# Wide-head attention without a loop, with queries, keys and values as split products

## What is computed

```python
DIM = 128; NUM_HEADS = 16; DIM_HEAD = 64; INNER = NUM_HEADS * DIM_HEAD      # 1024
w_q   (DIM, INNER)          queries from the twice normalised x
w_kv  (DIM, 2 * INNER)      keys and values from the context
w_out (INNER, DIM), b_out, gate, ln_gamma, ln_beta
...
def _layernorm(x, gamma, beta, eps=1e-05): ...
SCALE = DIM_HEAD ** (-0.5)
```

## Time and profile before

| | |
|---|---|
| median of 3 runs | 962.73 us (961.08 to 964.19) |
| span of the profiled execution | 1010.8 us |
| own time of the profiled execution | only the span is given |
| TensorE matmul busy | 783.2 us (77%) |
| VectorE busy | 608.2 us (60%) |
| ScalarE busy | 486.4 us (48%) |
| GpSimd busy | 372.9 us (37%) |

### The profile page before, as it was taken

One profiled execution on the slowest core, in us unless ns is written; L12 is line 12 of the kernel. 1 busy time (PEld: TensorE's weight loads), 2 busy tenths in 40 slices (PEclk: granted clock), 3 DMA queues, 4 the chain that ended last, 5 costly groups with the idle time before them and its releaser, 6 DMA issues.

```text
span 1010.8 us, 24129 instructions
## 1 busy us (share of the span) xinstructions
PE 783.2 (77%) x8041; PEld 646.4 (64%) x8041; DVE 608.2 (60%) x1568; ACT 486.4 (48%) x984; POOL 372.9 (37%) x492
## 2 busy tenths in 40 slices
PE   6998899999999789996477775667677559969005
PEld 3766787888888679985476664667676526644005
DVE  3886747777777667767353224632222368867895
ACT  3886434555444344432154435334444357745753
POOL 5663421111111331111566653155556535550810
PEclk9999699999999979999699989579989769978557
DMA  6300000000000000033332213101111300000001
GB/s 187 96 0 1 1 1 3 2 3 0 0 0 3 1 11 19 21 102 103 95 100 88 64 41 105 42 19 43 40 37 45 85 23 3 0 1 1 0 0 42
DMA packets 49218, 36.06 MB, mean 36 GB/s; under 512 B 7665, under 2 KB 44978, under 8 KB 49138
## 3 DMA queue, kind: packets, MB, share of 16 engines
q1 hardware_dynamic: 43420, 24.45, 8.5%
q0 software_dynamic: 4992, 10.23, 3.6%
q10 hardware_dynamic: 726, 0.33, 0.1%
HBM read 26.73 MB, written 8.26 MB: 35 GB/s over the span
## 4 chain that ended last, share of the span: by engine, by line
PE 67%; DVE 9%; another core or an unknown queue 6%; issue 5%; ACT 5%; DMA 3%; DVEq 2%; POOL 2%; ACTq 1%; SPq 1%; POOLq 0%
PE psum L2118 9%; PE psum L1464 7%; PE psum L2143 4%; PE psum L1034 3%; PE psum L976 3%; PE psum L954 3%; PE psum L939 3%; PE psum L2442 2%; PE psum L1431 2%; PE psum L1432 2%; PE psum L1433 2%; PE psum L323 2%; PE psum L1016 2%; PE psum L663 2%
## 5 line engine op out<-in xcount | busy, mean ns | idle before, releaser
L2118 PE MATMUL psum<-E_XT,E_weights 128*128 128x128 f32 x780 | 114.3, 298 | 52.4 <-ACT E_XT L2198 27.7
L2118 PEld LDWEIGHTS psum<-E_XT,E_weights 128*128 128x128 f32 x780 | 103.0, 209 | 61.2 <-ACT E_XT L2198 30.8
L2266 POOL DMA_INDIRECT y_scratch<-E_y,route_place_of x78 | 78.8, 1010 | 83.2 <-DVE E_y L2321 37.8
L2258 POOL DMA_INDIRECT E_rows<-rows_scratch,route_token_of x78 | 76.4, 979 | 32.1 <-issue 25.5
L1723 DVE SCALAR_TENSOR_TENSOR X<-psum,E_gates,X 128x128 f32<-128x128 f32 x256 | 71.7, 344 | 26.5 <-PE psum L1464 26.4
L1464 PEld LDWEIGHTS psum<-E_w,E_h 128*128 128x128 f32 x512 | 69.4, 198 | 11.5 <-issue 3.5
L2221 ACT ACTIVATE E_h<-psum,cols 128x128 f32<-128x128 f32 x156 | 44.5, 368 | 66.4 <-issue 31.3
L1548 ACT ACTIVATE E_h<-psum,cols 128x512 f32<-128x512 f32 x64 | 43.8, 687 | 67.8 <-PE psum L1433 67.7
L1464 PE MATMUL psum<-E_w,E_h 128*128 128x128 f32 x512 | 70.4, 282 | 4.8 <-DVE X L1723 3.8
L2311 DVE TENSOR_TENSOR E_h<-E_sg,psum 128x384 f32<-128x384 f32 x39 | 21.6, 554 | 77.5 <-remote 26.8
L203 POOL TENSOR_TENSOR rstd<-vareps,nhalf 128x4 f32<-128x4 f32 x24 | 24.6, 1029 | 75.0 <-DVE vareps L197 74.9
(11 more groups left out here) (346 smaller groups left out, 2160.2 us busy)
## 6 DMA issues: line engine op xcount, KB each, us to landing
routed_back<-y_scratch SPq DMA_DIRECT2D x16, 256.0 KB, 4.9
E_first<-in_L_xattn_W SPq DMA_DIRECT2D x1, 2048.0 KB, 8.6
L1w<-in_L_xattn_W SPq DMA_DIRECT2D x8, 256.0 KB, 4.7
rows_scratch<-xn SPq DMA_DIRECT2D x8, 256.0 KB, 2.3
E_w<-in_L_ffn_routed_w SPq DMA_DIRECT2D x28, 64.0 KB, 1.9
E_raw<-in_L_ffn_w_down SPq DMA_DIRECT2D x8, 176.0 KB
E_rows<-rows_scratch,route_token_of POOLq DMA_INDIRECT x78
y_scratch<-E_y,route_place_of POOLq DMA_INDIRECT x78
```

The costliest lines, as they stand in the source:

```text
L2118: mm = pe.matmul(out[:, c * P:(c + 1) * P], WE[:, p, (k0 + c) * P:(k0 + c + 1) * P], XT[:, p, :], start=True, stop=True)
L2258: pool.indirect_dma_start(out=xg[:, i % 4, :], out_offset=None, in_=rows[:, :], in_offset=bass.IndirectOffsetOnAxis(ap=disp.token_of[:, i: ...
L2266: pool.indirect_dma_start(out=yrows[:, :], in_=y[:, i % 3, :], in_offset=None, out_offset=bass.IndirectOffsetOnAxis(ap=disp.place_of[:, i: ...
```

## The change

The wide-head layer is written out for all its steps, without a hardware loop, and has 23 steps instead of 21. Keys, queries and values become products of three passes on split operands. Keys and queries are made for a pair of tiles: 256 moving columns, and of the eight blocks of 128 rows four in one step and four in the next (`half`). Values take the 128 context columns of both sequences as the stationary operand at once: 3 matmuls of 512 columns for each half of the heads. J1 then holds the even heads of both sequences and J0 the odd ones, and they are copied by halves of 64 partitions: two copies on VectorE, two on ScalarE.

The high and low parts come from four places. The weights: three copies of 128x1024 by ScalarE (`wide_high`) at the start of the feed-forward layer, and three subtractions by GpSimd (`low_parts`) in that layer, ahead of `owners`; the low part overwrites the weights. The context: four copies of 128x512 by ScalarE and four subtractions by GpSimd at the start of the wide-head layer, ahead of its first rstd. The normalised rows: a second evacuation of turn_x by ScalarE (xH) and a subtraction of 128x128 by GpSimd (xL, signal x_low), which takes the place of the context copy. The keys of the first pair stand ahead of the wait for the layer before. To make room, the weights of the feed-forward layer get a buffer of their own.

The diff, cut to its core:

```diff
+        def three(out, wk, cc, xs, start=True):
+            ws = slice(cc * P, (cc + 1) * P)
+            pe.matmul(out, WH[:, wk, ws], xs[0], start=True, stop=False)
+            pe.matmul(out, WH[:, wk, ws], xs[1], start=False, stop=False)
+            return pe.matmul(out, WL[:, wk, ws], xs[0], start=False, stop=True)
...
+        def turn_x(t, n, p):
+            pe.wait_ge(*xn_ready(t + 1))
+            if n >= 5:
+                pe.wait_ge(*v_odd(n - 4))
...
+        def queries(i, n):
+            pair, half = i // 2, i % 2
+            r = pair % 2
+            pe.wait_ge(*x_low(2 * pair + 2))
+            for j in range(2):
+                if 3 <= n <= NT:
+                    pe.wait_ge(*k_ready(2 * (n - 1) + j + 1))
...
+                for c in range(2):
+                    mm = three((J1, J0)[j][:, c * PW:(c + 1) * PW], 0, 4 * half + 2 * j + c, (xH[:, r, :], xL[:, r, :]))
+                mm.then_inc(q_ps.sem, 1)
...
+        def values(t, n):
...
+                pe.matmul(bank, CH[:, cols], wv[0][:, :, u, :], start=True, stop=False)
+                pe.matmul(bank, CL[:, cols], wv[0][:, :, u, :], start=False, stop=False)
+                mm = pe.matmul(bank, CH[:, cols], wv[1][:, :, u, :], start=False, stop=True)
...
+        for i in range(2):
+            keys(i, 0)
+        m.begin(pe, start)
+
         def step(n, p):
             q = 1 - p
...
+            if is_tile(n - 4):
+                scores(n - 4)
+            if is_tile(n - 1):
+                turn_x(n - 1, n, q)
+            if is_tile(n - 5):
+                turn_probs(n - 5, q)
...
+            if 3 <= n <= NT:
+                keys(n - 1, n)
+            if is_tile(n - 6):
+                turn_out(n - 6, p)
+            if is_tile(n - 2):
+                queries(n - 2, n)
+            if is_tile(n - 5):
+                weigh_values(n - 5, q)
...
+            if is_tile(n - 6):
+                project(n - 6, p)
+            if is_tile(n - 4):
+                values(n - 4, n)
...
     def scalar(act):
+        for s, n in first_products_done:
+            act.wait_ge(s, n)
+        for g in range(NG):
+            cols = slice(g * GW, (g + 1) * GW)
+            act.activation(CH[:, cols], m.ctxT[:, cols], ACT.Copy).then_inc(ctx_high.sem, 1)
...
+                act.wait_ge(*v_ps(2 * n - 6))
+                if n >= 6:
+                    act.wait_ge(*o_ps(n - 5))
+                for b in range(2):
+                    cp = act.activation(v[S:P, p, b].rearrange("p c d -> p (c d)"), J0[b * S:(b + 1) * S, :], ACT.Copy)
+                cp.then_inc(v_odd.sem, 1)
...
     def gpsimd(pool):
+        for g in range(NG):
+            cols = slice(g * GW, (g + 1) * GW)
+            pool.wait_ge(*ctx_high(g + 1))
+            pool.tensor_tensor(CL[:, cols], m.ctxT[:, cols], CH[:, cols], ALU.subtract).then_inc(ctx_low.sem, 1)
         m.begin(pool, start)
...
         def step(n, p):
-            if live(n):
+            if is_tile(n):
                 inner.rstd(pool, n, p, xn_ready)
-            if live(n + 1):
+            if is_tile(n + 1):
                 outer.rstd(pool, n + 1, 1 - p, x1_ready)
-            if live(n - 1):
-                context(n - 1, 1 - p)
+            if is_tile(n - 1):
+                t = n - 1
+                at = slice(t % 2 * P, (t % 2 + 1) * P)
+                pool.wait_ge(*xnT_ready(t + 1))
+                pool.tensor_tensor(xL[:, t // 2 % 2, at], xnT[:, 1 - p, :], xH[:, t // 2 % 2, at],
+                                   ALU.subtract).then_inc(x_low.sem, 1)
...
         if beside:
+            spec["pool_between"](pool)
             for j in range(NCH):
                 beside.owners(pool, j)
...
+        def low_parts(pool):
+            for i, k in enumerate((1, 0, 2)):
+                pool.wait_ge(wide_high_ready, i + 1)
+                pool.tensor_tensor(m.wide_low[:, k, :], wide[:, k, :], m.wide_high[:, k, :], ALU.subtract
+                                   ).then_inc(wide_low_ready, 1)
...
+            for k in (1, 0, 2):
+                act.activation(m.wide_high[:, k, :], wide[:, k, :], ACT.Copy).then_inc(wide_high_ready, 1)
```

More of the change, by code:

```diff
@@ L919, in wide_head_attention, with steps, is_tile @@
     L.done = x_done(NT)
[L920 to L927, removed]
+    END = NT + 7
+    first_products_done = m.split_free
+    after = m.stats_after.get
+    def steps(step):
+        for n in range(END):
+            step(n, n % 2)
+    def is_tile(t):
+        return 0 <= t < NT
     def tensor(pe):
-        m.begin(pe, start)
         pe.wait_ge(*m.dispatch.owner_ready(1))
-        def keys(t, p):
-            for j in range(2):
[L935 to L940, removed]
-                mm.then_inc(k_ps.sem, 1)
[L943 to L950, removed]
-                else:
[L952 to L955, removed]
-                mm.then_inc(v_ps.sem, 1)
[L958 to L983, removed]
@@ new lines, in step, with keys_kept @@
+            if after(tag) and n == NT + 5:
+                after(tag).turn(pe, 1)
+            if is_tile(n - 6):
+                project(n - 6, p)
+            if is_tile(n - 4):
+                values(n - 4, n)
+        steps(step)
+    def scalar(act):
+        for s, n in first_products_done:
[3 more added lines that the diff above has]
+            act.activation(CH[:, cols], m.ctxT[:, cols], ACT.Copy).then_inc(ctx_high.sem, 1)
+        def keys_kept(i):
+            pair, half = i // 2, i % 2
+            if pair >= 2:
+                act.wait_ge(*scores_ready(2 * pair - 2))
+            for j in range(2):
+                c = 4 * half + 2 * j
+                act.wait_ge(*k_ps(2 * i + j + 1))
+                act.activation(kT[pair % 2][:, c:c + 2, :].rearrange("p c k -> p (c k)"), (J1, J0)[j],
+                               ACT.Copy).then_inc(k_ready.sem, 1)
+        for i in range(2):
+            keys_kept(i)
@@ L1134, in gpsimd @@
         outer.rstd(pool, 0, 0, x1_ready)
[L1135 to L1136 removed]
+        steps(step)
+        if after(tag):
             for g in range(NG - 1):
[L1138 removed]
+                after(tag).rstd(pool, g)
             for g in range(2):
[L1140 to L1141 removed]
+                after(tag).low_part(pool, g)
+                after(tag).residual(pool, g)
     def vector(dve):
```

243 lines of the change are left out of this document (135 added, 108 removed).

## The result

The changed kernel takes 980.12 us (median of 4 runs, 979.38 to 983.59), the kernel before 963.15 beside it (961.08 to 964.19): ratio 1.0185, 95% interval 1.0154 to 1.0217, 17 us slower. Predicted were 977.5 (960 to 990), slower.

The account below looks back on a forecast made before the run. TensorE, busy all 11.70 us of a wide-head step, was taken to set that layer's pace. Collision 4.5 + filling 13.6 + clock 4.0 - steps 6.8 - last values 0.5 = +14.8 on 962.7: 977.5 us, range 960 to 990.

Parts of the forecast that it names:

- The collision (4.5): Feed-forward: GpSimd's weight subtractions hold VectorE's choice of experts, TensorE waits 4.5 us; 4.8 if reductions were held too.
- The new wait in even steps: Wide-head layer: queries wait for x_low, starting 8.46 us after project ended; an even step lasts 12.9.
- low part in time: Rival: x_low comes before turn_out ends, even steps last 10.5 us; 20.6 less, 956.9; chance 0.14.
- Its 8.6 for the start: Same rival, layer's filling: first queries 3.3 us earlier, third ones without a gap (2.6 + 2.7 less).
- Tile 2 to tile 15 (-6.8): From tile 2's scores to tile 15's: 144.1 us instead of 150.9, a gain of 6.8.
- The filling (13.6): Wide-head layer's start: late rstd and low parts put tile 2's scores at 187.0 instead of 173.43, 13.6 us lost.
- The last values (-0.5): After tile 15's scores: the last values give a gain of 0.5 us.
- The clock (4.0): Three new longer TensorE gaps lower the granted clock, 1.33 us lost at each: 4.0 in all, bound 6.7.
- The three gaps named: TensorE gaps before the table, before the first queries and before the third queries, expected to lower the clock.
- Split passes: Keys and queries: a pass of 256 columns costs 0.115 us, half of the 0.23 for 512.
- passes save nothing: Rival: a 256-column pass costs the 0.23 us of 512, 2.76 more per step; some 1000 us; chance 0.04.
- The loop: Wide-head layer written out without its loop: instruction loading costed at nothing, with the 23 straight steps as risk.

Follow-up runs that it names:

- dummy_subtract: Kernel before plus three GpSimd subtractions of 128x1024 on useless data, ahead of the owners: 969.6 us, ratio 1.0063 to the kernel before.
- dummy_fill: Kernel before plus three GpSimd fills of 128x3072 at the same place, ahead of the owners: 962.8 us, ratio 1.0000 to the kernel before.
- low_behind: Changed kernel with GpSimd's three subtractions for the weights' low parts moved behind its owners: 976.1 us, ratio 1.0133 to the kernel before.
- x_low_first: Changed kernel with GpSimd's subtraction for the queries' low part ahead of the next tile's outer rstd: 967.1 us, ratio 1.0030 to the kernel before.
- the odd half first: Changed kernel with x_low ahead of the rstd, weights split earlier on GpSimd, an earlier layer start, and the values' odd half first: 954.1 us, ratio 0.9901.
- unrolled: Kernel before with only its attention layer's loop of tiles 7 to 15 written out as straight steps: 960.6 us, ratio 0.9986.

## Why the prediction was right

**The collision (4.5).** Right in kind and size: TensorE waited 4.43. dummy_subtract shows the cause by itself. In dummy_fill, fills of 8.12 us, which only write, left the same operations alone; whether the reading or something else in a subtraction holds VectorE, these two runs by themselves do not separate. The reductions were not held, so 4.5 and not 4.8 was the right one of the two. The weights' high parts on ScalarE cost nothing here, as reckoned: low_behind has them and takes 42.16 in this stage, the kernel before 42.73.

**The new wait in even steps.** Right in kind, and x_low_first shows it. The chain from project's end to the queries took 8.1 (220.94 to 229.08) instead of 8.46 and an even step 12.63 to 12.75 instead of 12.9. The rival "low part in time" named the condition; once it was met, it gave 13 us, not 20.6. Its 12.0 for the steps was nearly right: from tile 2 to tile 15 x_low_first takes 11.4 less, with gaps of 1.6 to 1.9 instead of 2.4 and the 1.5 of step 6's clock on top. Its 8.6 for the start was too high: that stage fell by 4.4, since the first queries come 1.8 earlier and not 3.3 (they still wait 3.1), and the clock there stays low (0.50 in the first queries, 0.62 from 170.58 to the first scores). The stretch fell by 16.3 in all; the medians show 13.

**Tile 2 to tile 15 (-6.8).** This term was mis-sized: a gain of 2.8, not 6.8. Of the 4.0, steps 17 and 18 hold 2.5: they took 9.96 and 8.54 for 8.7 and 7.3, 0.89 of each a wait before turn_out for ScalarE's probabilities. The kernel before has that wait too, once, right behind its scores of tile 15, and I had left it out. The odd steps and step 16 hold 1.5: 10.74 for 10.5, six times, because the work is 10.46 and not 10.22. From start to start in TensorE's timeline of step 9, keys take 1.50 (237.54 to 239.04), queries 1.59 (239.83 to 241.42) and values 1.57 (244.32 to 245.89), together 4.66 for the 4.14 reckoned, and the rest takes 5.80 for 6.08. The first pass of each group, behind float32 work, costs 0.20 (224.90 to 225.10) where the next costs 0.12, and with 512 columns 0.31 (220.94 to 221.26) for 0.23; the last pass of queries and of values, ahead of matmuls of 64x64, costs some 0.09 more too (241.21 to 241.42). Step 6 at the lower clock took 14.38 for 13.5 (+0.9), and the four other even steps gave the same 0.9 back.

**The filling (13.6).** With the clock, 16.3 predicted and 15.5 measured. The first queries came 11.9 after GpSimd's last context part (it ended at 158.2), 12.0 reckoned; the first scores at 178.46 for 170.2, and 6.9 of that is the feed-forward's later end (150.69 for 143.77). Against the first profile, whose rows the sum used, the stage lost 17.0, so the term was 0.7 short rather than 0.8 long.

**The last values (-0.5).** They are 0.4 shorter (1.47 for 1.87), but TensorE then waits 0.41 for ScalarE's value copies (at 355.34), which I had left out: the stage shows +0.1. With the odd half first it falls to 27.3.

**The clock (4.0).** The three gaps named did drop it, and a fourth, of 1.89 in step 6. The cost is nearer 6.1 than 4.0: the rank products and second products took 2.3 longer, the 24 query passes of the two gaps in the filling 0.21 instead of 0.12 (2.3), step 6 1.5; it lies inside the stages above.

**Split passes.** 0.118 for 256 columns, 0.115 estimated; half of what 512 cost, so "passes save nothing" is out. **The loop.** Costed at nothing, and unrolled measures nothing.

So the sum came out 2.6 us below the measured median. In the stretch it was 4.3 short (19.1 for 14.8), 4.0 of it in the steps; that the total missed by less than the steps alone is chance, since this pair of profiles shows 2 us more than the medians. Open is why a gap of 1.89 dropped the clock in one run and one of 1.90 did not in another, and one of 1.76 in one of two executions of the same kernel; no run here tells them apart.

## What to carry to other kernels

An engine that is idle for most of a step can still set the pace: on an in-order engine, look at what stands ahead of the one instruction that others wait for, and put the instruction whose input comes first in front. When work is placed into an idle stretch of GpSimd, look at which VectorE instructions run beside it and what they read. And when a faster product does not shorten a step, compare TensorE's busy time with the window before judging the product: here 10.7 of work sat in steps of 12.6.

## What was not expected of the hardware

A GpSimd fill held a VectorE tensor_scalar of 128x8 for 2.07 us, though it left operations with two SBUF operands alone (0.29). It is one row; no run varies it. Going from a float32 product to float32r passes cost about 0.08 us each time, and going back to matmuls of 64x64 some 0.09. The three split groups of a step take 0.5 us more than their passes were priced at, though the float32 groups beside them take 0.3 less. And gaps of one length (1.76 us) ended at either level of the clock in two executions of one kernel.
